# Waves stage: gates folded into three copies of the output weights, their products summed in PSUM

## The reference

```python
v = _ln(x, ln2_g, ln2_b)
uu = (v @ W_si + b_si).reshape(b, s, H, DH)
up = jnp.pad(uu, ((0, 0), (2, 2), (0, 0), (0, 0)), mode='edge')
ux = (up[:, 3:-1] - up[:, 1:-3]) * 0.5
uxx = up[:, 3:-1] - 2.0 * uu + up[:, 1:-3]
uxxx = (up[:, 4:] - 2.0 * up[:, 3:-1] + 2.0 * up[:, 1:-3] - up[:, :-4]) * 0.5
sg = jnp.sin(uu)
kdv = -6.0 * uu * ux - uxxx
hj = (1.0 + alpha[None, None, :, None] * uu) * uxx
du = gates[..., 0:1] * sg + gates[..., 1:2] * kdv + gates[..., 2:3] * hj
sol = (SOL_DT * du).reshape(b, s, d) @ W_so + b_so
return x + sol
```

## Time and profile before

| | |
|---|---|
| median of 3 runs | 5562.75 us (5556.14 to 5563.07) |
| profiled execution, its time | 5562.39 us |
| profiled execution, its span | 5560.5 us |
| mean granted clock of TensorE | 0.954 |
| busy share of the span | PE 88%, PEld 50%, DVE 54%, ACT 40%, POOL 19% |
| waves stage, first matmul to end of last addition | 4110.04 to 4205.68 us from the span's start |

### The profile page before, as it was taken

The page is one execution under the profiler, slowest core; times in us unless marked ns, Lnnn a source line. Parts: engine busy times, 40 slices in busy tenths (PEclk is TensorE's granted clock), DMA queues, the critical chain, the costliest instruction groups (busy, mean ns, idle before and its releaser), DMA issues. The chain is left out here.

```text
span 5560.5 us, 89468 instructions
## 1 busy us (share of the span) xinstructions
PE 4891.6 (88%) x37194; PEld 2794.0 (50%) x37194; DVE 2998.5 (54%) x5854; ACT 2205.7 (40%) x3528; POOL 1063.4 (19%) x660
## 2 busy tenths in 40 slices
PE   6979996999999999999899995665637999999897
PEld 3468884666666666666444442232223333333465
DVE  5757773555455555555300006778766666666350
ACT  5734432444444444444211114555522544445421
POOL 0145552111011011000000003456541000000021
PEclk9989998999999999999999997899878999999898
DMA  2221111000000000000200000000001000000123
GB/s 87 103 92 49 49 45 41 9 7 27 7 10 18 15 7 21 7 10 4 85 0 0 0 0 28 0 0 0 0 5 39 1 13 1 13 1 1 56 80 105
DMA packets 45387, 144.14 MB, mean 26 GB/s; under 512 B 6928, under 2 KB 18768, under 8 KB 38240
## 3 DMA queue, kind: packets, MB, share of 16 engines
q1 hardware_dynamic: 43472, 134.55, 6.8%
q0 software_dynamic: 1536, 4.20, 0.2%
HBM read 102.69 MB, written 36.04 MB: 25 GB/s over the span
## 5 line engine op out<-in xcount | busy, mean ns | idle before, releaser
L1480 DVE CUSTOM_DVE_ANT_0 ma_prob<-ma_ring,ma_mask 128x400 f32<-128x400 f32 (+1 forms) x1024 | 527.4, 571 | 262.7 <-PE ma_ring L1584 262.7
L1932 DVE TENSOR_REDUCE fa_part<-fa_ring 128x1 f32<-128x512 f32 x768 | 486.6, 681 | 222.3 <-PE fa_ring L2053 203.4
L1879 ACT ACTIVATE fa_prob<-fa_ring 128x512 f32<-128x512 f32 (+1 forms) x832 | 441.6, 598 | 406.3 <-PE fa_ring L2053 328.4
L2053 PE MATMUL fa_ring<-fa_K,fa_Q 32*128 32x512 f32 (+1 forms) x2048 | 530.7, 546 | 2.0
L1493 DVE COPY ma_PT<-ma_ring 128x512 f32<-128x512 f32 x512 | 341.8, 688 | 287.3 <-PE ma_ring L1594 287.0
L1594 PE MATMUL ma_ring<-ident,ma_prob 128*128 128x128 f32 (+1 forms) x3328 | 462.1, 280 | 6.7 <-ACT ma_prob L1439 6.7
L2073 PE MATMUL fa_ring<-fa_Qm,fa_K 32*128 32x512 f32 (+1 forms) x1664 | 457.7, 629 | 2.3 <-DVE fa_Qm L1949 2.3
L1608 PE MATMUL ma_pv<-ma_PT,ma_V 128*64 128x256 f32 (+1 forms) x3328 | 457.8, 393 | 0.0
L2267 PE MATMUL ffn_mid<-ffn_hid,ffn_h 128*128 128x512 f32 x1024 | 441.5, 593 | 9.7 <-DVE ffn_hid L2233 6.3
L1406 POOL TENSOR_SCALAR ma_diag<-ident,ma_rtotal 128x128 f32<-128x128 f32 x256 | 149.7, 602 | 1535.5 <-DVE ma_rtotal L1498 1535.5
L1594 PEld LDWEIGHTS ma_ring<-ident,ma_prob 128*128 128x128 f32 (+1 forms) x3328 | 357.0, 141 | 163.6 <-issue 105.1
(11 more groups left out here) (377 smaller groups left out, 7823.4 us busy)
## 6 DMA issues: line engine op xcount, KB each, us to landing
gd_rows<-gp_tile SPq DMA_DIRECT2D x16, 1024.0 KB, 4.2
gd_c_vg<-gd_rows SPq DMA_DIRECT2D x16, 1024.0 KB
moe_w<-in_moe_w SPq DMA_DIRECT2D x16, 1024.0 KB, 7.0
ma_w<-in_ma_w SPq DMA_DIRECT2D x32, 384.0 KB, 3.1
gd_rows<-gp_gate SPq DMA_DIRECT2D x16, 512.0 KB, 5.1
gd_c_qk<-gd_rows SPq DMA_DIRECT2D x16, 512.0 KB
ffn_h<-in_ffn_h SPq DMA_DIRECT2D x2, 4096.0 KB, 22.7
ma_ctxT<-in_ctxT SPq DMA_DIRECT2D x4, 1601.0 KB, 7.0
```

Source lines behind the costliest of these rows:

```text
L1480: nc.vector.tensor_tensor_reduce(prob[:, u % 2, t, h, k0:k0 + width], bank("S", u, t, n, h)[:, 0:width], mask[:, b % 2, half * 2 + t, k0:k ...
L1879: nc.scalar.activation(prob[0:n, (u * KT + kt) % PROBS, j, :], bank("scores", u, kt, j)[0:n, :], ACT.Exp, scale=SCALE).then_inc(p_ready, 1)
L1932: ins = nc.vector.tensor_reduce(part[:, u % 2, t, j, n:n + 1], src[:], AX, ALU.max)
L2053: last = nc.tensor.matmul(bank("chunk", u, i)[:, at * w:(at + 1) * w], Q[rows, b % 2, g, tile * P:(tile + 1) * P], K[rows, b % 2, g, k0:k0 ...
```

## The change

`du` goes. A new tensor `w_gated` of shape `[P, 3, DC, D]` holds three copies of `wso`, each row multiplied by its channel's gate. VectorE makes it once at the start of its block, and TensorE waits for it before `inward(0)`. `outward(b)` multiplies `heat`, `sine` and `kdv` as they are by their copies and lets PSUM sum the six products of a token block. `combine(b)` keeps one instruction.

The reuse of buffers changes with it: `heat`, `sine` and `kdv` are now read by TensorE, so VectorE before `heat(b)`, ScalarE before `sine(b)` and GpSimd before `kdv(b)` wait for the `out_ready` of batch b - 2. `take(b)` waits for `heat_ready` in place of `du_ready`.

```diff
-        angle, sine, d1, d2, f, kdv, heat, du = (wide(n) for n in (...))
+        angle, sine, d1, d2, f, kdv, heat = (wide(n) for n in (...))
+        w_gated = s.sb("w_gated", [P, 3, DC, D])
...
             def outward(b):
-                pe.wait_ge(du_ready, b + 1)
+                pe.wait_ge(heat_ready, b + 1)
+                pe.wait_ge(sine_ready, b + 1)
+                pe.wait_ge(wave_ready, b + 1)
                 if b >= 2:
                     pe.wait_ge(added, 2 * (b - 1))
                 for t in range(TB):
-                    for k in range(DC):
-                        last = nc.tensor.matmul(out_ps[b % 2][t // 2][:, t % 2, :], du[:, b % 2, k, t * P:(t + 1) * P], wso[:, k, :],
-                                                start=(k == 0), stop=(k == DC - 1))
+                    terms = [(g, term, k) for g, term in ((2, heat), (0, sine), (1, kdv)) for k in range(DC)]
+                    for i, (g, term, k) in enumerate(terms):
+                        last = nc.tensor.matmul(out_ps[b % 2][t // 2][:, t % 2, :], term[:, b % 2, k, t * P:(t + 1) * P],
+                                                w_gated[:, g, k, :], start=(i == 0), stop=(i == len(terms) - 1))
                     if t % 2 == 1:
                         last.then_inc(out_ready, 1)
 
+            pe.wait_ge(w_ready, 1)
             inward(0)
...
             def take(b):
                 act.wait_ge(u_ready, b + 1)
                 if b >= 2:
-                    act.wait_ge(du_ready, b - 1)
+                    act.wait_ge(heat_ready, b - 1)
                     act.wait_ge(kdv_ready, b - 1)
...
             def take_sine(b):
                 act.wait_ge(angle_ready, b + 1)
                 if b >= 2:
-                    act.wait_ge(du_ready, b - 1)
+                    act.wait_ge(out_ready, 2 * (b - 1))
...
                 pool.wait_ge(up_ready, b + 1)
-                if b >= 2:
-                    pool.wait_ge(du_ready, b - 1)
                 nc.gpsimd.tensor_tensor(d1[:, k], at(b, 3), at(b, 1), ALU.subtract)
                 chain.link(nc.gpsimd.tensor_scalar(f[:, k], at(b, 2), -3.0, 1.0, ALU.mult, ALU.add))
+                if b >= 2:
+                    pool.wait_ge(wave_ready, b - 1)
+                    pool.wait_ge(out_ready, 2 * (b - 1))
                 chain.link(nc.gpsimd.tensor_tensor(kdv[:, k], f[:, k], d1[:, k], ALU.mult))
...
+            for g in range(3):
+                for k in range(DC):
+                    last = nc.vector.tensor_scalar(w_gated[:, g, k, :], wso[:, k, :], gates[:, g, k:k + 1], None, ALU.mult)
+            last.then_inc(w_ready, 1)
...
                 nc.vector.scalar_tensor_tensor(out=s1[:], in0=at(b, 2), scalar=-2.0, in1=s1[:], op0=ALU.mult, op1=ALU.add)
+                if b >= 2:
+                    dve.wait_ge(out_ready, 2 * (b - 1))
                 for m in range(DC):
                     last = nc.vector.tensor_scalar(heat[:, k, m, :], up[:, k, m, EDGE:EDGE + T], alpha[:, m:m + 1], 1.0,
                                                    ALU.mult, ALU.add)
                 chain.link(last)
-                chain.link(nc.vector.tensor_tensor(heat[:, k], heat[:, k], s1[:], ALU.mult))
+                nc.vector.tensor_tensor(heat[:, k], heat[:, k], s1[:], ALU.mult).then_inc(heat_ready, 1)
 
             def combine(b):
                 k = b % 2
                 dve.wait_ge(kdv_ready, b + 1)
-                chain.link(nc.vector.scalar_tensor_tensor(out=kdv[:, k], in0=d2[:, k], scalar=-0.5, in1=kdv[:, k],
-                                                          op0=ALU.mult, op1=ALU.add))
-                dve.wait_ge(sine_ready, b + 1)
-                for m in range(DC):
-                    chain.link(nc.vector.tensor_scalar(sine[:, k, m, :], sine[:, k, m, :], gates[:, 0, m:m + 1], None, ALU.mult))
-                for g, term in ((1, kdv), (2, heat)):
-                    for m in range(DC):
-                        last = nc.vector.scalar_tensor_tensor(out=du[:, k, m, :], in0=term[:, k, m, :], scalar=gates[:, g, m:m + 1],
-                                                              in1=(sine if g == 1 else du)[:, k, m, :], op0=ALU.mult, op1=ALU.add)
-                    if g == 1:
-                        chain.link(last)
-                last.then_inc(du_ready, 1)
+                nc.vector.scalar_tensor_tensor(out=kdv[:, k], in0=d2[:, k], scalar=-0.5, in1=kdv[:, k],
+                                               op0=ALU.mult, op1=ALU.add).then_inc(wave_ready, 1)
```

More of the change, by code:

```diff
@@ L2742, in waves @@
         wide = lambda n: s.sb(n, [P, 2, DC, T])
-        angle, sine, d1, d2, f, kdv, heat, du = (wide(n) for n in ("angle", "sine", "d1", "d2", "f", "kdv", "heat", "du"))
+        angle, sine, d1, d2, f, kdv, heat = (wide(n) for n in ("angle", "sine", "d1", "d2", "f", "kdv", "heat"))
+        w_gated = s.sb("w_gated", [P, 3, DC, D])
         turns = s.sb("turns", [P, DC, T])
@@ L2754, in waves @@
         kdv_ready = s.sem("kdv_ready")
-        du_ready = s.sem("du_ready")
+        heat_ready = s.sem("heat_ready")
+        wave_ready = s.sem("wave_ready")
+        w_ready = s.sem("w_ready")
         out_ready = s.sem("out_ready")
```

## The result

The changed kernel takes 5574.99 us (median of 8 runs, 5567.59 to 5579.71), the kernel before 5559.75 (8 runs beside them). The ratio is 1.0027, 95% interval 1.0018 to 1.0036: slower, by 15 us, with 10 and 20 us at the interval's ends. The profiled executions have spans of 5573.9 and 5560.5 us, 13.4 apart.

A forecast was written before the change was run, and what follows sets the result against it. VectorE was taken to set the stage's pace. Later entry, new waits and longer product bursts moved the stage's end from 4205.68 to 4218.4, +12.8 us; against the 5562.75 median that gave 5575.5 us, range 5566 to 5584.

The forecast's parts named there:

- a ring over TensorE and VectorE: Rounds of the stage become a chain over two engines: product, then `heat` and `combine`, then product.
- entry, TensorE starts later: At the stage's start TensorE waits for VectorE's gates and six scalings, so it starts 2.2 us later.
- first burst at half clock: `inward(0)`, after the longer entry pause, may run at half clock: 2.4 us taken, bounds 0 and 3.5.
- `shape(1)` and `combine(0)` with GpSimd beside them: VectorE's work before `outward(0)`: 9.15 and 1.26 us, plus 2.3 for GpSimd's `d1(2)` and `f(2)` beside it.
- `outward(0)` to `heat(2)`: `outward(0)`, now 24 products for 8, takes 12.6 us, and `heat(2)` waits for its end.
- VectorE idle before `heat(2)`: VectorE waits 5.6 us before `heat(2)` for the `out_ready` of batch 0.
- `heat(2)` to `outward(1)`: `heat(2)` and `combine(1)`, with GpSimd's `kdv(2)`, `d2(2)` and `d1(3)` beside them, take 8.6 us before `outward(1)`.
- `outward(1)` to `heat(3)`: `outward(1)` takes 12.1 us: 5.42 us from the row before, plus 6.6 for sixteen more products.
- last two bursts with the addition: At the stage's end the last two bursts run as one with 32 more products: 23.3 us, plus 0.73 for the addition.
- The signs that I named: Expected in the changed profile: start and length of `outward(0)`, VectorE idle before `heat(2)`, `outward` spacing, last burst, first `take`.
- Rival (a): VectorE remains the bound and the products hide beneath it, only the last burst bare: -7.0 us, 5555.8; chance 0.05.
- another pause of 4.3 us: Row from 4120.7 to 4125.0 where TensorE's clock held, cited as evidence that the entry's longer pause might be free.

The follow-up runs named there:

- x2: The changed kernel with a third buffer for `sine`, `kdv` and `heat`, so their waits for `out_ready` point one batch further back; 5568.10 us, ratio 1.0015.
- x3: The changed kernel with `combine(1)` and `combine(2)` moved ahead of `heat(2)` and `heat(3)` and their wait for the products; 5566.52 us, ratio 1.0010.
- x4: The kernel before, with each product of `outward` issued three times, VectorE's work and all waits as before; 5574.32 us, ratio 1.0026.
- x1: The changed kernel with TensorE's wait for the gated weights moved from before `inward(0)` to before `outward(0)`; 5572.40 us, ratio 1.0023.
- x9: The changed kernel with five products, later overwritten, on TensorE ahead of its wait for the gated weights; 5573.73 us, ratio 1.0021.
- x5: The changed kernel with only the `kdv` term projected; sine and heat still computed but left out of the output; 5551.27 us, ratio 0.9987.
- x6: The changed kernel with the edits of x1, x2 and x3 together; 5561.90 us, ratio 1.0003.
- x10: The changed kernel with GpSimd's `d2` moved ahead of its wait for `out_ready`, `kdv` behind it; 5567.60 us, ratio 1.0012.
- x7: x6 with all four `inward` issued first and batch 3 gated and summed on VectorE as before the change; 5551.97 us, ratio 0.9989.

## Why the prediction was right

Forecast: 5575.5 us, slower, by a ring over TensorE and VectorE. Measured: 5574.99. The sum's steps against the trace:

| step | forecast | measured |
|---|---|---|
| entry, TensorE starts later | 2.2 | 2.01 |
| first burst at half clock | 2.4 | 1.50 |
| `shape(1)` and `combine(0)` with GpSimd beside them | 12.7 | 12.67 |
| `outward(0)` to `heat(2)` | 12.6 | 12.29 |
| VectorE idle before `heat(2)` | 5.6 | 5.47 |
| `heat(2)` to `outward(1)` | 8.6 | 8.79 |
| `outward(1)` to `heat(3)` | 12.1 | 13.68 |
| `heat(3)` to `outward(2)` | 7.0 | 7.20 |
| last two bursts with the addition | 24.0 | 24.53 |
| stage against before | +12.8 | +13.5 |

**Mechanism and number.** The mechanism is shown: VectorE's new idle time and the ring (x2, x3), and the two bare bursts at the end (x4). That the time was hit to 0.5 us is luck beside that. The forecast was 12.8 us above 5562.75, the median of three runs; eight runs have 5559.75, 3.0 lower, and the difference is +15.2, 2.4 more than forecast. These two nearly cancel. Of the stage's +13.5, too, the terms up to `outward(0)` are 1.4 us below the forecast and those behind it 2.2 above.

**The signs that I named.** `outward(0)` starts 1.5 us later, counted from the entry, and not 2 to 4; it takes 12.1 us to where `inward(3)` follows (12 to 13.5 named). Of the 3.5 us of the first two rows 3.2 arrive at the start of `shape(1)`, for 4.6. The idle time before `heat(2)` is there, ended by TensorE, and again before `heat(3)`, 5.66 us. The starts lie 21.08 and 20.88 us apart (19 to 22). The last bursts take 23.8 us, counted to the last addition (23 named). The first `take` is 3.5 us later (2.2 to 5.7). The rest of the program has the same length.

**Terms that were off.** The first burst: 1.5 for 2.4, as the clock was back by 4115, 3.5 us into it. `outward(1)`: 13.7 for 12.1, the largest miss. I had taken its slow start from the 5.42 us of one row; here the clock stood at 0.50 until past 4179, over 5.8 us into the burst. The two misses have opposite signs and partly cancel. Both sizes hang on where in a burst the clock comes back, and that moves: x1, x9 and the change have the same program from `outward(0)` on and the same pause of 5.39 us before `outward(1)`, and the first two take 1.4 and 1.3 us less in this round.

**A rival that was mispriced.** Rival (a), VectorE stays the bound, was priced at -7.0 with 6.6 us for "the last burst is bare". x4 shows that two bursts are bare, +12.45. And its 15.8 counts four batches, though `combine(3)` lay beside `outward(2)` in the kernel before too; only three are on the path, 11.9. With both mended the rival comes to -11.9 + 2.2 + 12.4 = +2.7: no change, and not faster. (The rounds of x5 gained 12.4 us and not 7.9, as `up` also came earlier and GpSimd cost less there, so such a sum is good to some 5 us.) So a step of my own sum ("the two run as one with 32 more products") was right, and the same step was left out of the rival. It also means that even without the ring, and with all four batches in this form, the change could not have won much: x6, which also has x1's earlier start, has 1.0003.

**The rule on pauses.** The longer pause at the entry did cost. The clock stood at 0.92 in the mean over 4109.4 to 4111.4 and at 0.50 from 4111.5; x9, which only fills the pause, has 1.00 throughout and gets 1.36 us back. This is what the Trainium skill (TensorE: Matmul & The Clock Gate, Why this matters for your kernels) advises, and here the trace agrees with it. The prediction set against this "another pause of 4.3 us" in which the clock held. That row was misread: it is the first part of a pause of 30.56 us, and in the kernel before the clock fell right behind it, to 0.67 in the mean of the next microsecond:

```profile
4125.00:4126.00 1.00, 0.00 (x0) 0.00 (x0) 0.96 (x2) 0.00 (x0) 1.00 (x1) 0.67 0.00 0
```

So no pause of that length ended at full clock there. What the traces do show is that the clock outlasts a burst by a varying time: it was still at 1.00 some 4.4 us behind the burst that ended at 4120.6, and no longer at 4163, 2.3 us behind the one that ended at 4160.7. The value of 2.4 us for the first burst, which also rests on "the later case is the commoner", was an estimate that no count of cases stood behind.

**What stays open.** Each kernel has one profiled execution, so how much of a difference of 1 to 2 us between two of them is the clock's return falling elsewhere was not tried by repeating one. Nor were x3 and x10 put together, so how much of their gains is the same is not known; together they cannot be read as 18 us, since both shorten the same chain, and the combination cost 12.8.

## What to carry to other kernels

Before work is moved from a bound engine to an idle one, ask how long a result then stays in its buffer: three terms read by TensorE in place of one sum made it a releaser of buffers, and what stood behind the new waits without needing them could be moved ahead, and that gave back 9.7 us on one queue (x3) and 9.0 on the other (x10), each tried by itself. And price the end of a stage apart from its rounds: products hidden in a round are bare behind the last wait, so the last batch can be worth another form than the others (x7).

## What the hardware showed that I had not expected

- A pause of TensorE is paid again in the burst behind it, and in a ring that lengthens the next wait. Behind 2.1 us `outward(1)` took 10.7 us to `heat(3)` (x10), behind 5.4 us 13.7, for the same 24 products (48 records).
- The burst behind a pause did not have one price. Behind the same pause of 5.39 us `outward(1)` was slow for about 3 us in x1 and over 5.8 us in the change. A term of this kind deserves both ends in a range, not one row.
- Two queues released by one event run beside each other exactly. In the change `kdv(2)` and `heat(2)` are, and GpSimd's `kdv(2)`, `d2(2)` and `d1(3)` each meet one step of VectorE and lengthen it by 2.1, 1.6 and 1.7 us (2.98 for 0.87, 2.80 for 1.23, 2.91 for 1.22). The Trainium skill has the two engines share a port pair that one instruction holds for its whole length (SBUF — State Buffer, SBUF: two separate sides), and the rows agree: the three VectorE instructions end at 4167.38, 4170.21 and 4173.04, each behind the end of GpSimd's (4167.09, 4169.13, 4171.96). What I had not expected is how much hangs on the last of the three, which `take(3)` releases: in the change `d1(3)` starts 0.6 us before `combine(1)`, in x10 0.96 us after it, and misses it.
